# Closer chains for sequences 0 to 3, and a GpSimd list that scatters sequence 3's rows ahead of the gathers for sequences 4 to 7

## What is computed

```python
x = x + 0.5 * ffn(layernorm(x))     # first MoE pass
x = x + attn(layernorm(x))
x = x + 0.5 * ffn(layernorm(x))     # second MoE pass, same weights

def ffn(x):                         # 12 experts, 3 for each token
    topw, sel = top_k(x @ Wg, 3);  topw = softmax(topw)
    y = gelu(x @ Wup[e] + bup[e]) @ Wdown[e] + bdown[e]      # for each expert e
    return sum of topw * y over the three chosen experts

def attn(x):                        # for each sequence by itself
    u = silu(x @ Wg + bg) * (x @ Wi + bi)
    y = Cp * (causal convolution of u with Bp * A**t) + Dp * u
    y = layernorm(y) * gamma + beta
    return (silu(y @ Wfg + bfg) * (y @ Wfu + bfu) @ Wfd + bfd) @ Wo + bo
```

## Time and profile before

| | |
|---|---|
| median of 3 runs | 625.49 us (623.89, 625.49, 630.26) |
| span of the profiled execution | 623.9 us |
| PE busy | 560.0 us, 90% |
| ACT busy | 514.5 us, 82% |
| POOL busy | 416.4 us, 67% |
| DVE busy | 373.2 us, 60% |

### The profile page before, as it was taken

The page is one execution under the profiler, slowest core; times in us unless marked ns, Lnnn a source line. Parts: engine busy times, 40 slices in busy tenths (PEclk is TensorE's granted clock), DMA queues, the critical chain, the costliest instruction groups (busy, mean ns, idle before and its releaser), DMA issues.

```text
span 623.9 us, 17393 instructions
## 1 busy us (share of the span) xinstructions
PE 560.0 (90%) x4527; PEld 522.7 (84%) x4527; DVE 373.2 (60%) x1735; ACT 514.5 (82%) x1462; POOL 416.4 (67%) x424
## 2 busy tenths in 40 slices
PE   7559879999999999999899799998798799999995
PEld 6449779999999888878889688787698799999992
DVE  7947788653111577888865679987828532232224
ACT  3557777599998989899889699998589679998984
POOL 1074557677776777327677777777777777777770
PEclk9999988899999999999999799999799989999997
DMA  7996242343454343312255333332264532433264
GB/s 192 323 222 190 63 113 67 86 123 87 128 161 128 104 119 101 80 45 67 72 169 133 90 87 98 90 98 70 69 153 109 131 87 70 117 87 83 61 225 136
DMA packets 99127, 72.28 MB, mean 116 GB/s; under 512 B 13520, under 2 KB 91910, under 8 KB 99033
## 3 DMA queue, kind: packets, MB, share of 16 engines
q1 hardware_dynamic: 83032, 43.62, 25.5%
q0 software_dynamic: 13024, 26.11, 14.9%
q10 hardware_dynamic: 2976, 1.44, 0.9%
HBM read 37.08 MB, written 34.75 MB: 115 GB/s over the span
## 4 chain that ended last, share of the span: by engine, by line
PE 38%; DVE 15%; POOL 14%; issue 11%; DMA 11%; ACT 6%; SPq 3%; ACTq 1%; DVEq 1%; POOLq 0%
PE ps L1001 16%; PE ps L1014 15%; POOL YG L807 11%; DMA yk<-Ys,row 4%; DMA YG<-ys,SY 3%; ACT hT L1184 2%; POOL yk L818 2%; DVE YG L1698 2%; SPq L607 1%; PE ps L971 1%; DVE X L1311 1%; DVE st L1255 1%; DVE Ys L2037 1%; PE ps L961 1%; DMA xl<-xna,SG 1%
## 5 line engine op out<-in xcount | busy, mean ns | idle before, releaser
L1184 ACT ACTIVATE hT<-ps,BU 128x128 f32<-128x128 f32 x900 | 260.5, 390 | 52.8 <-PE ps L1001 42.0
L1014 PE MATMUL ps<-WD,hT 128*128 x1800 | 245.0, 281 | 18.8 <-DVE Ys L2037 18.7
L1001 PE MATMUL ps<-xT,WT 128*128 128x128 f32 x1800 | 248.7, 283 | 5.9 <-ACT xT L1174 3.0
L1014 PEld LDWEIGHTS ps<-WD,hT 128*128 128x128 f32 x1800 | 224.6, 196 | 22.2 <-issue 22.1
L1001 PEld LDWEIGHTS ps<-xT,WT 128*128 128x128 f32 x1800 | 228.5, 198 | 15.3 <-issue 11.7
L790 POOL DMA_INDIRECT xs<-XN,SX x144 | 146.6, 1018 | 64.6 <-issue 58.1
L807 POOL DMA_INDIRECT YG<-ys,SY x132 | 135.6, 1027 | 43.3 <-issue 35.3
L2037 DVE TENSOR_TENSOR Ys<-ps,BD 128x128 f32<-128x128 f32 x225 | 63.9, 288 | 165.9 <-PE ps L1014 158.5
L1067 ACT ACTIVATE WT<-WU 128x512 f32 x225 | 149.9, 667 | 7.0 <-DVE eW L1731 3.5
L818 POOL DMA_INDIRECT yk<-Ys,row x71 | 70.9, 999 | 21.7 <-issue 12.5
L777 POOL DMA_INDIRECT xl<-xna,SG x24 | 24.3, 1013 | 40.9 <-DMA xna<-XN 27.4
(11 more groups left out here) (366 smaller groups left out, 583.8 us busy)
## 6 DMA issues: line engine op xcount, KB each, us to landing
ys<-Ys SPq DMA_DIRECT2D x41, 256.0 KB
xl<-xs SPq DMA_DIRECT2D x94, 64.0 KB
xl<-xs SPq DMA_DIRECT2D x71, 66.0 KB
WU<-in_L_ffn_Wup_dram SPq DMA_DIRECT2D x12, 256.0 KB, 5.0
WD<-in_L_ffn_Wdown_dram SPq DMA_DIRECT2D x12, 256.0 KB, 5.2
YG<-yk SPq DMA_DIRECT2D x4, 768.0 KB, 7.6
xs<-XN,SX POOLq DMA_INDIRECT x144
YG<-ys,SY POOLq DMA_INDIRECT x132
```

The costliest lines, as they stand in the source:

```text
L1001: x = e.matmul(HB[i % 2][:, c * P:(c + 1) * P], WT[i % NW][:, c, :], xT[m % 2][:, j * P:(j + 1) * P], start=True, stop=True)
L1014: x = e.matmul(YB[i % 2][:, 0:D], hT[i % 3][:, c * P:(c + 1) * P], WDf[:, bass.ds(r + c * P, P)], start=(c == 0), stop=(c == C - 1))
L1184: x = e.activation(hT[i % 3][:, c * P:(c + 1) * P], HB[i % 2][:, c * P:(c + 1) * P], ACT.Gelu, bias=BU[:, bass.ds(b + c, 1)])
```

## The change

The slots of sequences 0 to 3 in `CHAIN` move earlier by up to 7; the slots of sequences 4 to 7 stay. Sequence 3 moves most: its `T` goes from slot 48 to 44, its `L` from 50 to 45, its `N` on ACT from 50 to 46, and its `K` from 53 to 46. So `K` of sequence 3 now stands in the last slot of phase 1 instead of the seventh of phase 2. In the list `POOL`, the entry `("K", 3)` moves from behind `("Y", 7)` to ahead of `("Y", 4)`. Nothing is added or removed. Some lines of the diff:

```diff
-    ("V", "G0", (8, 13, 19, 27, 54, 58, 65, 72)),
+    ("V", "G0", (8, 13, 19, 25, 54, 58, 65, 72)),
...
-    ("A", "N", (31, 38, 44, 50, 75, 81, 85, 89)),
-    ("PV", "K", (33, 38, 44, 53, 75, 81, 86, 89)),
+    ("A", "N", (28, 35, 41, 46, 75, 81, 85, 89)),
+    ("PV", "K", (30, 36, 42, 46, 75, 81, 86, 89)),
 ]
-POOL = (("Y", 0), ("Y", 1), ("Y", 2), ("Y", 3), ("K", 0), ("K", 1), ("K", 2), ("Y", 4), ("Y", 5), ("Y", 6), ("Y", 7),
-        ("K", 3), ("K", 4), ("K", 5), ("K", 6), ("K", 7))
+POOL = (("Y", 0), ("Y", 1), ("Y", 2), ("Y", 3), ("K", 0), ("K", 1), ("K", 2), ("K", 3), ("Y", 4), ("Y", 5),
+        ("Y", 6), ("Y", 7), ("K", 4), ("K", 5), ("K", 6), ("K", 7))
```

## The result

| | before | after |
|---|---|---|
| median of 4 runs | 625.15 us (623.89 to 630.26) | 652.54 us (651.43 to 653.95) |
| span of the profiled execution | 623.9 us | 651.7 us |
| PE busy | 560.0 us | 567.9 us |
| DVE busy | 373.2 us | 373.3 us |
| last `Ys` of phase 2 ends | 462.58 us | 491.61 us |

The kernel became slower: the ratio is 1.0436, with a 95% interval of 1.0399 to 1.0473. The prediction was 634.7 us in a range of 628 to 641. So the direction was right, and the size was off by a factor of three: 27.4 us instead of 9.2.

What follows compares the result with a forecast made beforehand. PE and ACT were taken to bound phase 1, then POOL's gathers until 360 us, then the engines. Span 623.9 + 12.0 us of later gathers - 2.0 us back = 633.9, as a median 634.7 us; range 628 to 641.

Steps and rivals of the forecast that it cites:

- What the scatters of sequence 3 cost ahead of the gathers: On POOL at the border of phases 1 and 2: twelve scatter issues ahead of sequence 4's gathers take 15.5 us.
- What the delay does: Phase 2: gathers 12.0 us late keep their spacing, DVE's waits stay, and the whole 12.0 us reach the phase's end.
- later waits swallow the delay: Rival: DVE's 6.35 us of waits for gathers of sequences 4 and 5 come off; 628.4 us as a median; chance 8%.
- What comes back: Phase 3: POOL's list runs ahead without the scatter backlog, giving back 2.0 us, bounds 0 and 4.67.
- The sum's own base: Span of 623.9 us, taken as the lowest run, plus 0.8 us to forecast a median.
- Moved work makes the tile later: Phase 1's last tile: sequence 3's moved steps delay it 2.2 us by ACT's share, bounds 0 and DVE's 6.46.
- The start of sequence 3's scatters: POOL behind slot 46: start at 319.9 + 2.2 = 322.1 us, end at 337.6, first gather for sequence 4 12.0 us later.
- That `K` of sequences 0 to 2 comes earlier costs nothing and hardly helps: POOL in phase 1: its idle time before 276.45 covers earlier scatters; the possible 2.7 us gain goes to sequence 3's scatters.
- DVE paces phase 1: Rival: DVE's queue grows and phase 1's last tile is 6.5 us late; 638.2 us, up to 640.5; chance 11%.
- Slot 46 comes early: Rival: closer chains fill PE's waits in phase 1, so scatters start at 314.2; 626.8 us as a median; chance 12%.
- The scatters did not stretch: Rival that sequence 3's twelve scatters slow beside other traffic to 27.1 us, 11.6 more; 645.5 us; chance 3%.
- What would show it: Trace signs: scatters end near 337, DVE waits 11 to 13 us at sequence 4's `G0`, POOL hole about 12 us.

Runs made afterwards that it cites:

- the list alone: Kernel before with only the change's POOL list, `K` of sequence 3 ahead of the `Y` entries, slots as before: 650.54 us, ratio 1.0385.
- three numbers: Kernel before with sequence 0's `A3` in slot 17 instead of 18, `S3` and `S3'` in 18 instead of 19: 631.01 us, ratio 1.008.
- the columns of sequences 0 to 2: Kernel before with the change's slots for sequences 0, 1 and 2; sequence 3's column and POOL's list as before: 630.92 us, ratio 1.0095.
- sequence 3's column up to `A7`: Kernel before with the change's slots of sequence 3 from `G0` to `A7` only; `T` to `K` and POOL's list as before: 642.05 us, ratio 1.0251.
- its front: Kernel before with the change's slots of sequence 3 for `G0` to `C3` only: 631.85 us, ratio 1.0111.
- its rear: Kernel before with the change's slots of sequence 3 for `A3` to `A7` only: 634.93 us, ratio 1.0165.
- sequence 3's column by itself: Kernel before with the change's whole column of sequence 3, `T` to `K` included, and the POOL list of before: 641.83 us, ratio 1.0254.
- the order of two steps on DVE: Changed kernel with `S1` of sequence 1 again ahead of `S3` and `S3'` of sequence 0 in slot 18: 648.83 us, ratio 1.0348.
- the line on PSUM banks: Changed kernel with that `S1` order, and a bank that `L` used counted as free one slot later: 643.22 us, ratio 1.029.

## Why the prediction was wrong, step by step

*What the scatters of sequence 3 cost ahead of the gathers* was right: 15.5 us taken, 15.63 measured. POOL took 0.98 us for most of these issues, with DVE busy 6.37 of 15.70 us beside them:

```profile
339.70:355.40 15.70, 15.69 (x140) 15.48 (x139) 6.37 (x24) 14.61 (x45) 12.00 (x13) 1.00 0.40 115
```

The port rule of the Trainium skill (SBUF — State Buffer, section "A bandwidth-pool intuition that's wrong") would make an issue about five times as long beside a DVE copy that holds the port; no row here shows such an issue, nor whether DVE held it.

*What the delay does* was right: the delay reaches DVE at `G0` of sequence 4, the waits behind it did not shrink (5.22 and 3.11 us, against 3.42 and 2.73), and 29.0 of 29.8 us reach the end of phase 2. The rival that later waits swallow the delay falls. That the wait at `G0` has the size forecast, 11.98 us, is chance: the gathers are 29.8 us late instead of 12.0, and DVE gets there 16.9 us later itself (352.66 against 335.73).

*What comes back* was taken as 2.0 us and is 29.0 - 27.8 = 1.2 us of span, with the wait of `F0` at 3.63 instead of 4.67 us. The hole on POOL behind the gathers is there, 13.47 us.

*The sum's own base* was short by 0.9 us. A run's time is its span and 1.7 to 1.8 us more: the profiled execution after the change has a span of 651.7 and a time of 653.55 us, and with the list alone it is 649.3 and 651.04. I took the span of 623.9 us for the lowest of the three times and added 0.8; of the three times only 625.49 us comes near this span plus 1.7.

*Moved work makes the tile later* is the step that failed. I took 2.2 us, and 6.5 as the upper bound; slot 47 begins 18.1 us later. The sentence that failed with it is "All other moves stay inside phase 1", which priced them at nothing, with idle time as their cover. The runs show the opposite. Moves inside the phase make it late with nothing moved in: three numbers 4.6 us, the columns of sequences 0 to 2 7.6 us, sequence 3's column up to `A7` 15.9 us, its front and its rear 10.3 and 8.2 us. They don't add up: the whole change costs 17.4, less than the 23.5 of its two sets of columns, and why was not followed. That the moved work adds nothing is shown for sequence 3's column by itself; for the whole change it is not, since no kernel has all four columns with `T` to `K` of sequence 3 left behind. Two single causes were taken out: the order of two steps on DVE gave back 2.9 us, and the line on PSUM banks, with the picks that it changes, 1.9 to 4.5 us by slot 46. Beyond these, one stop (`A1` of sequence 3) was followed to its cause; where the rest goes is open.

Idle time was no cover: a moved step fills a gap only where it stands just ahead of an instruction that waits. In the two stops that were followed it stands ahead of a step that could have run, and makes that one later by its length, less the slack that the other had, and the slack could be read before: 0.2 us at 231.96, against 3.2 us of moved steps, and none at `C2` of sequence 2, where ACT waited already, against 2.2 us. The upper bound was wrong for the same reason: work that one engine has more is no bound for what three engines wait for each other.

*The start of sequence 3's scatters* was tied to slot 46, with 322.1 us; their rows were ready at 336.8, when the cast into `SX` ended, but POOL was with sequence 2's scatters until 339.74. The prediction said "That `K` of sequences 0 to 2 comes earlier costs nothing and hardly helps", and took for granted that it does. That POOL works through its list in order, and that sequence 2's scatters are the last thing ahead, was in the earlier trace rows: I looked at the entry that moved, not at the one ahead of it.

*The rivals.* "DVE paces phase 1" came nearest, by the place, but DVE wasn't short of time: it idles 12.7 us more. "Slot 46 comes early" asked for closer chains to fill PE's idle time; they raise it by 11.0 us. The scatters did not stretch.

*What would show it* held by half: "If the scatters start later than 326, the moved work has cost more than I took." They start at 339.74, but what cost the time was not the moved work.

## What to carry to other kernels

Where engines run fixed orders, a step that is moved is priced at every place it passes: its length, less the slack between the result that it is put ahead of and the engine that takes it, counts as a wait, and one such wait for DVE can become one on ACT and then a stop of PE, as twice here. An engine's idle time is no cover for it. For a list that one engine works off, look at what stands ahead of the moved entry, and find the one start that the end follows: here a single gather, with the end of the phase 136 to 139 us behind it in 15 of 16 kernels beside the one before.

## What was not expected of the hardware

A stop of PE can cost more than its length. Right behind the stop of 3.45 us the eight products of line 1001 took 1.92 us (PE's row at 238.41 above), and just before it 1.06 us:

```profile
231.66 1.06 PE L1001 MATMUL ps<-xT,WT 128*128 128x128 f32 x8
```

Behind the stop the granted clock is 0.50:

```profile
238.00:242.00 4.00, 4.00 (x20) 4.00 (x20) 0.27 (x2) 4.00 (x13) 3.02 (x4) 0.50 0.19 51
```

The granted clock of the stretch below, about slots 19 to 29 after the change, is 0.89, and 1.00 for the same slots before:

```profile
231.00:276.00 45.00, 36.08 (x242) 30.87 (x241) 29.99 (x146) 34.15 (x91) 20.94 (x21) 0.89 0.22 60
```

```profile
230.40:264.00 33.60, 32.38 (x245) 28.06 (x244) 27.11 (x115) 31.32 (x87) 20.59 (x21) 1.00 0.34 89
```

PE is busy 36.08 instead of 32.38 us for nearly the same instructions (242 and 245 in the trace), so of 11.4 us more, 3.7 are slower products and 7.7 idle time. Behind DVE's wait of 11.98 us the granted clock of 355 to 375 us is 0.66:

```profile
355.00:375.00 20.00, 8.68 (x53) 8.31 (x51) 5.06 (x23) 5.38 (x16) 15.19 (x16) 0.66 0.29 76
```

The Trainium skill (TensorE: Matmul & The Clock Gate, section "What's actually happening") names two levels, 1.2 and 2.4 GHz, and the lower for an array that was idle; the rows agree, with 0.50 against 1.00 granted and 1.92 against 1.06 us for eight products. The lower clock doesn't follow every stop: of the two above, 2.47 and 2.48 us long and with the same instructions around them, one had it behind it and the other had not. The prediction had no term for it.
